# Three layer norms in a retention and mixture-of-experts kernel: rows broadcast ahead of the gate projection, a bf16 normalisation fed by POOL's casting loads, and an output normalisation on DVE alone

## The chip, the cores and the metric

The kernel runs on 8 cores of one Trainium2 chip. Every core works on 2048 tokens of its own and the cores exchange nothing. The metric is the device time of the slowest core in microseconds (us).

## What is computed

One layer: a linear retention with 16 heads, its layer norm and gate, then a mixture of 8 experts. Each half ends in a layer norm over the 2048 features. Cut to what matters:

```python
q = x @ Wq.T;  v = x @ Wv.T                    # heads of 128
ret = scan(state = lam * state + v)            # along the sequence
out = _layernorm(q * ret, gamma, beta)         # "LN1"
x1 = x + (out * silu(x @ Wg.T)) @ Wo.T
x1n = _layernorm(x1)                           # "LN2"
w = top-2 of sigmoid(x1n @ Wgate.T), normalised
h = silu(x1n @ W1[e].T) * (x1n @ W3[e].T) * w[:, e]     # 8 experts
out = _layernorm(x1n + sum_e h @ W2[e].T)      # "LN3"
```

The kernel adds in the last line what it keeps in `x1hbm`, x1 before its norm.

## The kernel before

Tokens lie along the free axis and features on the 128 partitions, so one core's 2048 tokens make 16 feature tiles. The work is done in two halves of 1024 tokens (`emit_half`, called twice), and each half in two chunks of 512 (`c`, `CW=512`). The program is written out as five lists of instructions, one for each engine, in the order in which Python emits them. Each engine runs its list in order and waits on semaphores. Nothing reorders them, so the place of a call in the source is its place in each engine's queue. POOL's queue carries both POOL's arithmetic and the loads that convert f32 to bf16; SP's queue carries plain loads and the stores of x1, ACT's the stores of the output.

A half goes through these stages:

- POOL loads all 16 tiles of `xnS` from `xfm` (line 471). `xnS` is first the bf16 input x, later the normalised x1.
- Wv (L492) and Wq (L563), 16 column groups each, 32 matmuls to a group. Weights come through `wringS`, a ring of 4 column tiles that `load_wcol` fills from POOL's queue (L226). ACT copies the Wv result out of PSUM banks 0 and 1 (L519), DVE runs the scan (L539) and multiplies (L575).
- LN1 statistics: sums and sums of squares by matmuls against a column of ones (L601, L609).
- `ln_rows` (L379 to L409): for each chunk, five short DVE instructions on one partition, a square root on ACT and a DVE reciprocal. It fills the rows `muR` and `rstdR`, 1x1024 each.
- Gate projection Wg: 16 groups (L631), silu on ACT into `ygS` (L644).
- `bcast_rows` (L423, L434; copies L429, L440): a matmul with a row of ones spreads each row over 128 partitions, and DVE copies it into `muB` and `rstdB`. It is called after the gate projection.
- DVE normalises: for each of 16 heads and 2 chunks one subtract (L658) and two multiplies (L664, L672), into `ygS`.
- Wo: 16 groups (L703), each reading all 16 tiles of `ygS`. DVE adds x (L716) from `xf32S` (loaded on SP, L690) into `x1tS`, which SP stores to `x1hbm` (L725). Statistics follow (L749, L758). `xf32S` and `x1tS` are rings of 4 tiles of 512.
- LN2: `ln_rows`, `bcast_rows`, then SP reloads x1 in f32 (L778), and a subtract (L784) and a multiply (L791) per tile and chunk write `xnS`, even tiles on DVE, odd ones on POOL. An all-engine barrier follows.
- Router (L833 and after), then four pairs of experts: W1 (L948), W3 (L966), W2 (L1020), with the sum kept in `x2S`.
- LN3: statistics (L1083, L1092), `ln_rows`, `bcast_rows`, then subtract (L1110) and multiply (L1117) per tile and chunk into `ot2S` (4 slots), even tiles on DVE, odd ones on POOL. ACT's queue stores the output (L1124).

Two waits matter at the seam between the halves. The `xnS` loads of the second half wait for the last read of `xnS` by W3, through `xn_b`; they stand in POOL's list behind whatever POOL has to do before them. And ACT's copy out of PSUM (L519) stands in ACT's list behind the 32 output stores.

Of the kernel before, what the change touches and what calls it, by code (L numbers as in the profile page):

```python
# [26 lines left out]
class Prog:  # L27

    def __init__(self, nc):
        self.nc = nc  # L30
# [4 lines left out]
        names += [f"dG{i}" for i in range(4)] + [f"dR{i}" for i in range(4)]
        names += [f"dW{i}" for i in range(4)] + [f"dA{i}" for i in range(2)]
        names += [f"out{i}" for i in range(4)]
        for s in names:
            self.sems[s] = nc.alloc_semaphore(s)
            self.counts[s] = 0  # L40
# [80 lines left out]
def build(TC=2048, PREF=6144, CW=512):  # L121
# [72 lines left out]
    xf32S = A("xf32S", [P, 4 * CW], F32)  # L194
# [19 lines left out]
    xfR = Ring(4)  # L214
    x1R = Ring(4)
# [4 lines left out]
    gbufB = [[Buf() for _ in range(FT)] for _ in range(2)]  # L220

# [195 lines left out]
    def bcast_rows(t_mu, t_rs, bank_a, bank_b):
        dmu = muB_b.begin_write()
        drs = rstdB_b.begin_write()
        toks = []  # L420
        for c in range(NCW):
            da = psB[bank_a].begin_write()
            tm = pr.tick("pe", lambda en, c=c, b=bank_a: en.matmul(  # L423
                out=psS[b][:, 0:CW], lhsT=onesrow_f[:],
                rhs=muR[:, c * CW:(c + 1) * CW], start=True, stop=True),
                deps=[t_mu[c], t_ones_f] + da + dmu)
# [16 lines left out]
            psB[bank_b].read(tbr)  # L443
            toks += [tbm, tbr]
# [8 lines left out]
    def emit_half(half, state_prev_half):  # L453
# [3 lines left out]
        with (  # L457
# [7 lines left out]
            nc.sbuf_tensor(f"x1tS{half}", [P, 4 * CW], F32) as x1tS,  # L465
# [153 lines left out]
            t_mu1, t_rs1 = ln_rows(st_sum + st_sq, 0, 2)  # L619
# [32 lines left out]
            bt1 = bcast_rows(t_mu1, t_rs1, 4, 5)  # L652
# [116 lines left out]
            t_mu2, t_rs2 = ln_rows(st2_sum + st2_sq, 4, 6)  # L769
            bt2 = bcast_rows(t_mu2, t_rs2, 6, 7)  # L770
# [3 lines left out]
            for kt in range(KT):  # L774
                eng = "dve" if kt % 2 == 0 else "pool"
                for c in range(NCW):
                    xslot, xbuf = xfR.next()
                    trb = pr.dma("sp", lambda en, kt=kt, c=c, xslot=xslot: en.dma_start(  # L778
                        out=xf32S[:, xslot * CW:(xslot + 1) * CW],
                        in_=x1hbm[kt * P:(kt + 1) * P, hoff + c * CW:hoff + (c + 1) * CW]),  # L780
                        deps=t_x1w_all + xbuf.begin_write(), sem=f"dR{xslot}")
                    xbuf.wrote(trb)
                    ntslot, ntbuf = ntR.next()
                    tn1 = pr.tick(eng, lambda en, xslot=xslot, c=c, ntslot=ntslot: en.tensor_tensor(  # L784
                        out=ntmpS[:, ntslot * CW:(ntslot + 1) * CW],
# [448 lines left out]
```

How the kernel before makes its waits and increments, by code:

```python
            def run(engobj):  # L70
                lastwait = {}
                for deps, action, inc, inc_by in self.steps[eng]:
                    for s, v in deps:
                        if lastwait.get(s, 0) < v:
                            engobj.wait_ge(self.sems[s], v)
                            lastwait[s] = v
                    ins = action(engobj)
                    if inc is not None:
                        ins.then_inc(self.sems[inc], inc_by)
```

## Time and profile before

| | us |
|---|---|
| median of 2 runs | 4744.77 (4743.55 to 4746.0) |
| the profiled execution | 4743.55 |
| its span on the slowest core (core 7) | 4741.9 |
| spans of the eight cores | 4731.9 to 4741.9 |
| PE busy | 3961.9 (84%) |
| DVE busy | 1210.7 (26%) |
| POOL busy | 510.3 (11%) |
| ACT busy | 351.2 (7%) |

The span runs from the first to the last instruction of a core; the profiled execution's time is 1.65 us above it. Busy shares are means over stages that have different limits. What the change touches lies in the short stretches in which PE stands still, so the views to read are the chain that ended last and the timeline at each of those stretches.

### The profile page before, as it was taken

What the parts mean: (1) busy time and instruction counts of PE and PEld (TensorE: products, weight loads), DVE (VectorE), ACT (ScalarE), POOL (GpSimd) and SP (SyncE); (2) the same over time, 40 slices, a digit from 0 to 9 for tenths busy, and PEclk for the clock granted to TensorE, in tenths of its full rate; (3) what the DMA queues carried; (4) which work ended last, traced back from release to release, by engine and by line L of the source; (5) the groups of instructions that cost most, each with busy time, mean ns of one, the idle gap of its engine ahead of it and who ended that gap; (6) DMA issues with size and microseconds to landing.
All of it is one profiled execution on the core that took longest, in us unless ns stands there. A gap on an engine that the chain in (4) does not pass through costs nothing.

```text
span 4741.9 us, 46603 instructions; the slowest of 8 cores (4731.9 to 4741.9 us)
## 1 busy us (share of the span) xinstructions
PE 3961.9 (84%) x17449; PEld 1698.8 (36%) x17449; DVE 1210.7 (26%) x1891; ACT 351.2 (7%) x622; POOL 510.3 (11%) x730
## 2 busy tenths in 40 slices
PE   5698848189999999999919984736999999999993
PEld 1243313034444444444404431312444444444441
DVE  0122061621211211112242216152121121121126
ACT  0002101000000000000100210100000000000001
POOL 2100000400000000000050000030000000000004
PEclk5699969599999999999959996967999999999996
DMA  9843325334744444444254331533465444444441
GB/s 161 132 74 53 65 53 133 102 58 71 137 80 71 78 72 71 72 71 76 49 124 76 67 54 28 136 115 58 71 113 99 71 78 71 72 76 71 72 75 71
DMA packets 132169, 388.99 MB, mean 82 GB/s; under 512 B 15216, under 2 KB 15216, under 8 KB 131952
## 3 DMA queue, kind: packets, MB, share of 16 engines
q0 software_dynamic: 85392, 302.06, 38.6%
q1 hardware_dynamic: 37344, 67.17, 4.8%
q10 hardware_dynamic: 9216, 16.78, 1.0%
q8 instruction: 147, 2.41, 0.2%
q14 instruction: 70, 0.57, 0.0%
HBM read 654.42 MB, written 33.55 MB: 145 GB/s over the span
## 4 chain that ended last, share of the span: by engine, by line
PE 79%; DVE 8%; DMA 4%; issue 4%; POOL 3%; ACT 2%; DVEq 0%; ACTq 0%; POOLq 0%; SPq 0%; PEldq 0%
PE ps L948 19%; PE ps L1020 19%; PE ps L966 19%; PE ps L631 5%; PE ps L492 5%; PE ps L563 5%; PE ps L703 4%; DMA wring<-xpre 2%; DMA wring<-wvT 1%; DVE ntmpS L664 1%; DVE ygS L672 1%; POOL ot2S L1110 1%; DVE x1tS L716 1%; DVE ntmpS L658 1%; PE ps L925 1%
## 5 line engine op out<-in xcount | busy, mean ns | idle before, releaser
L948 PE MATMUL ps<-xnS,wring 128*128 128x512 bf16 x4096 | 939.4, 389 | 0.0
L966 PE MATMUL ps<-xnS,wring 128*128 128x512 bf16 x4096 | 904.9, 379 | 0.0
L1020 PE MATMUL ps<-gbufS,wring 128*128 128x512 bf16 x4096 | 886.4, 379 | 0.0
L948 PEld LDWEIGHTS ps<-xnS,wring 128*128 128x128 bf16 x4096 | 407.6, 100 | 526.6 <-issue 66.7
L966 PEld LDWEIGHTS ps<-xnS,wring 128*128 128x128 bf16 x4096 | 400.8, 98 | 483.2
L1020 PEld LDWEIGHTS ps<-gbufS,wring 128*128 128x128 bf16 x4096 | 400.2, 98 | 484.9 <-issue 3.5
L989 DVE TENSOR_TENSOR gtmpS<-ps,sh1S 128x512 bf16<-128x512 f32 x256 | 175.9, 687 | 1470.1 <-PE ps L966 1470.1
L703 PE MATMUL ps<-ygS,wring 128*128 128x512 bf16 x1024 | 258.0, 409 | 122.8 <-DVE ygS L672 122.8
L492 PE MATMUL ps<-xnS,wring 128*128 128x512 bf16 x1024 | 231.3, 385 | 106.7 <-DMA wring<-wvT 106.7
L982 ACT ACTIVATE sh1S<-ps 128x512 bf16<-128x512 f32 x256 | 139.0, 594 | 2366.9 <-PE ps L948 2366.9
L631 PE MATMUL ps<-xnS,wring 128*128 128x512 bf16 x1024 | 236.6, 385 | 48.1 <-ACT ygS L644 30.9
L1045 DVE SCALAR_TENSOR_TENSOR x2S<-ps,x2S 128x512 f32<-128x512 f32 x192 | 132.8, 692 | 517.5 <-PE ps L1020 517.5
L563 PE MATMUL ps<-xnS,wring 128*128 128x512 bf16 x1024 | 226.2, 379 | 0.0
L703 PEld LDWEIGHTS ps<-ygS,wring 128*128 128x128 bf16 x1024 | 99.1, 101 | 276.5 <-issue 177.9
L492 PEld LDWEIGHTS ps<-xnS,wring 128*128 128x128 bf16 x1024 | 101.2, 99 | 232.6 <-issue 115.0
L998 DVE TENSOR_TENSOR gbufS<-ewbS,gtmpS 128x512 bf16<-128x512 f32 x256 | 177.2, 692 | 27.7 <-DVE gtmpS L989 1.4
L226 POOL DMA_DIRECT2D wring<-w1T x128 | 67.7, 529 | 999.3 <-PE ps L948 924.6
L631 PEld LDWEIGHTS ps<-xnS,wring 128*128 128x128 bf16 x1024 | 99.0, 99 | 185.3 <-issue 78.7
L226 POOL DMA_DIRECT2D wring<-w2T x128 | 67.5, 528 | 817.6 <-PE ps L1020 613.1
L226 POOL DMA_DIRECT2D wring<-w3T x128 | 67.6, 528 | 801.6 <-PE ps L966 701.7
L563 PEld LDWEIGHTS ps<-xnS,wring 128*128 128x128 bf16 x1024 | 98.9, 98 | 117.1
L328 PE MATMUL ps<-wring,preWb 128*16 128x512 bf16 x192 | 88.4, 614 | 60.7 <-DMA wring<-xpre 57.6
(130 smaller groups left out, 1655.7 us busy)
## 6 DMA issues: line engine op xcount, KB each, us to landing
wring<-w1T POOLq DMA_DIRECT2D x128, 512.0 KB, 5.1
wring<-w3T POOLq DMA_DIRECT2D x128, 512.0 KB, 5.1
wring<-w2T POOLq DMA_DIRECT2D x128, 512.0 KB, 5.0
xf32S<-x1hbm SPq DMA_DIRECT2D x128, 256.0 KB, 3.7
wring<-xpre POOLq DMA_DIRECT2D x48, 512.0 KB, 9.8
xf32S<-xfm SPq DMA_DIRECT2D x64, 256.0 KB, 6.9
wring<-wvT POOLq DMA_DIRECT2D x32, 512.0 KB, 6.1
wring<-wqT POOLq DMA_DIRECT2D x32, 512.0 KB, 6.1
```

The lines of the kernel that those rows point to most:

```text
L226: lambda en, t=wringS[s], sr=src_ap, X=X: en.dma_start(out=t[:, 0:X], in_=sr),
L492: grp = pr.step("pe", lambda en, kt=kt, c=c, slot=slot: en.matmul(out=psS[c][:, 0:CW], lhsT=wringS[slot][:, kt * P:(kt + 1) * P], rhs=xqS[ ...
L563: grp = pr.step("pe", lambda en, kt=kt, c=c, slot=slot: en.matmul(out=psS[2 + c][:, 0:CW], lhsT=wringS[slot][:, kt * P:(kt + 1) * P], rhs= ...
L631: grp = pr.step("pe", lambda en, kt=kt, c=c, slot=slot: en.matmul(out=psS[c][:, 0:CW], lhsT=wringS[slot][:, kt * P:(kt + 1) * P], rhs=xqS[ ...
L703: grp = pr.step("pe", lambda en, kt=kt, c=c, slot=slot: en.matmul(out=psS[2 + c][:, 0:CW], lhsT=wringS[slot][:, kt * P:(kt + 1) * P], rhs= ...
L948: g1 = pr.step("pe", lambda en, kt=kt, c=c, slot=slot1: en.matmul(out=psS[c][:, 0:CW], lhsT=wringS[slot][:, kt * P:(kt + 1) * P], rhs=x1nS ...
L966: g3 = pr.step("pe", lambda en, kt=kt, c=c, slot=slot3: en.matmul(out=psS[2 + c][:, 0:CW], lhsT=wringS[slot][:, kt * P:(kt + 1) * P], rhs= ...
L982: ts1 = pr.tick("act", lambda en, c=c, shslot=shslot: en.activation(out=sh1S[:, shslot * CW:(shslot + 1) * CW], in_=psS[c][:, 0:CW], func= ...
L989: tg1 = pr.tick("dve", lambda en, c=c, shslot=shslot, gtslot=gtslot: en.tensor_tensor(out=gtmpS[:, gtslot * CW:(gtslot + 1) * CW], in0=psS ...
L998: gd = pr.tick("dve", lambda en, ei=ei, ft=ft, c=c, gtslot=gtslot: en.tensor_tensor(out=gbufS[:, (ei * FT + ft) * TH + c * CW:(ei * FT + f ...
L1020: grp = pr.step("pe", lambda en, k=k, c=c, slot=slot2: en.matmul(out=psS[4 + c][:, 0:CW], lhsT=wringS[slot][:, k * P:(k + 1) * P], rhs=gbu ...
L1045: tx2 = pr.tick("dve", lambda en, ht=ht, c=c: en.scalar_tensor_tensor(out=x2S[:, ht * TH + c * CW:ht * TH + (c + 1) * CW], in0=psS[4 + c][ ...
```

## The change

`ln_rows` and `bcast_rows` become one function, `ln_rows_bcast`, that works chunk by chunk: rows of the chunk, its two broadcast matmuls, its two copies, then the next chunk. The rows shrink from 1x1024 to 1x512, so chunk 1 waits until chunk 0's matmuls have read them. For LN1 it is called before the gate projection instead of `ln_rows` there and `bcast_rows` behind. LN2 and LN3 now broadcast through banks 2 and 3.

LN2's normalisation reads x1 as bf16: POOL's queue loads it with conversion into `xcS` (ring of 4), two DVE casts make bf16 copies of `muB` and `rstdB`, and subtract and multiply run on DVE alone, all operands bf16. LN3's normalisation runs on DVE alone, still in f32. `xf32S` and `x1tS` go from 4 slots to 3.

```diff
+    def ln_rows_bcast(stat_toks, bank_sum, bank_sq, bank_a, bank_b):
...
         for c in range(NCW):
+            rowdep = rowsB.begin_write()
             tmu = pr.tick("dve", lambda en, c=c: en.tensor_scalar(
-                out=muR[:, c * CW:(c + 1) * CW],
-                in0=psS[bank_sum + c][0:1, 0:CW],
+                out=muR[:, 0:CW], in0=psS[bank_sum + c][0:1, 0:CW],
                 scalar1=1.0 / D, scalar2=None, op0=ALU.mult),
                 deps=list(stat_toks) + rowdep)
...
-            t_mu1, t_rs1 = ln_rows(st_sum + st_sq, 0, 2)
+            bt1 = ln_rows_bcast(st_sum + st_sq, 0, 2, 4, 5)
...
             xn_b.read(g_grp[NH - 1])
-            bt1 = bcast_rows(t_mu1, t_rs1, 4, 5)
...
+            bt2 = ln_rows_bcast(st2_sum + st2_sq, 4, 6, 2, 3)
+            t_mbb = pr.tick("dve", lambda en: en.tensor_copy(
+                out=muBb[:, 0:TH], in_=muB[:, 0:TH]), deps=bt2 + muB_b.begin_write() * 0)
+            t_rbb = pr.tick("dve", lambda en: en.tensor_copy(
+                out=rstdBb[:, 0:TH], in_=rstdB[:, 0:TH]), deps=bt2)
...
-                eng = "dve" if kt % 2 == 0 else "pool"
-                    trb = pr.dma("sp", lambda en, kt=kt, c=c, xslot=xslot: en.dma_start(
-                        out=xf32S[:, xslot * CW:(xslot + 1) * CW],
+                    trb = pr.dma("pool", lambda en, kt=kt, c=c, xcslot=xcslot: en.dma_start(
+                        out=xcS[:, xcslot * CW:(xcslot + 1) * CW],
                         in_=x1hbm[kt * P:(kt + 1) * P, hoff + c * CW:hoff + (c + 1) * CW]),
...
-                eng3 = "dve" if ht % 2 == 0 else "pool"
+                eng3 = "dve"
```

On PE, from the last LN1 statistics of the first half to the first Wo group, the four broadcast matmuls (`ps<-muR`, `ps<-rstdR`) stand behind the gate projection in the kernel before:

```order
L609 MATMUL ps<-sqS,onescol_bf 1x512
L631 MATMUL ps<-xnS,wring 128x512 x512
L423 MATMUL ps<-muR,onesrow_f 128x512
L434 MATMUL ps<-rstdR,onesrow_f 128x512
L423 MATMUL ps<-muR,onesrow_f 128x512
L434 MATMUL ps<-rstdR,onesrow_f 128x512
L703 MATMUL ps<-ygS,wring 128x512 x32
```

In the changed kernel they stand ahead of it (its own line numbers; L622 is the gate projection, L693 is Wo):

```order
L599 MATMUL ps<-sqS,onescol_bf 1x512
L412 MATMUL ps<-muR,onesrow_f 128x512
L423 MATMUL ps<-rstdR,onesrow_f 128x512
L412 MATMUL ps<-muR,onesrow_f 128x512
L423 MATMUL ps<-rstdR,onesrow_f 128x512
L622 MATMUL ps<-xnS,wring 128x512 x512
L693 MATMUL ps<-ygS,wring 128x512 x32
```

The gate's 512 matmuls moved behind both chunks' broadcast, and Wo follows them directly.

On POOL, at the seam between the halves, the kernel before has 32 LN3 instructions (16 such pairs, then line 471) between the last W2 loads and the next half's input:

```order
L226 DMA wring<-w2T 128x2048 x16
L1110 TENSOR_TENSOR ot2S<-x2S,muB 128x512
L1117 TENSOR_TENSOR ot2S<-ot2S,rstdB 128x512
L1110 TENSOR_TENSOR ot2S<-x2S,muB 128x512
L1117 TENSOR_TENSOR ot2S<-ot2S,rstdB 128x512
```

In the changed kernel the same place reads (L461 is the load of the input):

```order
L233 DMA wring<-w2T 128x2048 x16
L461 DMA xnS<-xfm 128x1024 x16
L233 DMA wring<-wvT 128x2048
L233 DMA wring<-wqT 128x2048
L233 DMA wring<-wvT 128x2048
L233 DMA wring<-wqT 128x2048
```

Nothing is left between the last W2 load and the second half's input.

On DVE, for LN1, the kernel before has the two copies of each chunk behind both chunks' rows:

```order
L409 RECIPROCAL rstdR<-rstdR 1x512
L379 TENSOR_SCALAR muR<-ps 1x512
L386 TENSOR_SCALAR msR<-ps 1x512
L392 TENSOR_TENSOR rstdR<-muR 1x512
L396 TENSOR_TENSOR msR<-msR,rstdR 1x512
L401 TENSOR_SCALAR msR<-msR 1x512
L409 RECIPROCAL rstdR<-rstdR 1x512
L429 COPY muB<-ps 128x512
L440 COPY rstdB<-ps 128x512
L429 COPY muB<-ps 128x512
L440 COPY rstdB<-ps 128x512
```

In the changed kernel chunk 0's copies come before chunk 1's rows (L418 and L429 are the copies):

```order
L409 RECIPROCAL rstdR<-rstdR 1x512
L418 COPY muB<-ps 128x512
L429 COPY rstdB<-ps 128x512
L387 TENSOR_SCALAR muR<-ps 1x512
L392 TENSOR_SCALAR msR<-ps 1x512
L397 TENSOR_TENSOR rstdR<-muR 1x512
L400 TENSOR_TENSOR msR<-msR,rstdR 1x512
L403 TENSOR_SCALAR msR<-msR 1x512
L409 RECIPROCAL rstdR<-rstdR 1x512
L418 COPY muB<-ps 128x512
L429 COPY rstdB<-ps 128x512
```

The DVE list is as long as before here; only two copies moved forward.

## Rows read from the trace of the kernel before

**Rows 1.** The page, part 4: shares of the chain that ended last, by engine.
```profile
PE 79%; DVE 8%; DMA 4%; issue 4%; POOL 3%; ACT 2%; DVEq 0%; ACTq 0%; POOLq 0%; SPq 0%; PEldq 0%
```
**Rows 2.** Waits: who waited for whom, us in total, times, longest.
```profile
PE ps L703 <- DVE ygS L672: 122.8, 32, 5.7
```
**Rows 3.** Timeline, start of the first half's gate projection: start us, us, engine, line.
```profile
443.55 0.68 DVE L379 TENSOR_SCALAR muR<-ps 1x512 f32<-1x512 f32 x1 [20.21 <-PE ps L609]
...
448.83 3.34 DVE L409 RECIPROCAL rstdR<-rstdR 1x512 f32<-1x512 f32 x1 [2.10 <-ACT rstdR L405]
452.10 0.62 DVE L379 TENSOR_SCALAR muR<-ps 1x512 f32<-1x512 f32 x1
...
452.96 8.39 PE L631 MATMUL ps<-xnS,wring 128*128 128x512 bf16 x31 [8.11 <-DVE muR L379]
...
456.03 3.34 DVE L409 RECIPROCAL rstdR<-rstdR 1x512 f32<-1x512 f32 x1 [0.82 <-ACT rstdR L405]
```
**Rows 4.** Timeline, LN2's broadcast matmul of the first half.
```profile
843.94 2.04 PE L434 MATMUL ps<-rstdR,onesrow_f 1*128 1x512 f32 x2 [6.44 <-DVE msR L386]
```
**Rows 5.** Timeline, last gate group of each half.
```profile
579.73 5.56 PE L631 MATMUL ps<-xnS,wring 128*128 128x512 bf16 x25
...
2862.38 7.23 PE L631 MATMUL ps<-xnS,wring 128*128 128x512 bf16 x32 [0.94 <-ACT ygS L644]
```
**Rows 6.** The chain in order of time, Wo groups: start us, us, what.
```profile
670.54 9.03 PE ps L703 x32
682.90 7.03 PE ps L703 x32
693.40 7.03 PE ps L703 x32
...
2958.49 8.53 PE ps L703 x32
```
**Rows 7.** Timeline, LN2's normalisation: its first DVE instructions and POOL's last.
```profile
855.01 0.68 DVE L784 TENSOR_TENSOR ntmpS<-xf32S,muB 128x512 f32<-128x512 f32 x1
...
856.41 0.68 DVE L784 TENSOR_TENSOR ntmpS<-xf32S,muB 128x512 f32<-128x512 f32 x1
...
909.01 1.26 POOL L791 TENSOR_TENSOR xnS<-ntmpS,rstdB 128x512 bf16<-128x512 f32 x1
```
**Rows 8.** Groups by line: busy us, mean ns, idle before.
```profile
L791 DVE TENSOR_TENSOR xnS<-ntmpS,rstdB 128x512 bf16<-128x512 f32 x32 | 48.3, 1509 | 3.3
...
L732 DVE CAST cbS<-x1tS 128x512 bf16<-128x512 f32 x64 | 27.3, 427 | 6.6
...
L316 DVE CAST preWb<-preW 128x768 bf16<-128x768 f32 x1 | 0.6, 560 | 2.2 <-ACT preW L311 2.2
```
**Rows 9.** DMA issues: out<-in, queue, count, KB written by each, median us to landing.
```profile
xf32S<-x1hbm SPq DMA_DIRECT2D x128, 256.0 KB, 3.7
...
wring<-wgT POOLq DMA_DIRECT2D x32, 512.0 KB, 5.1
wring<-woT POOLq DMA_DIRECT2D x32, 512.0 KB, 7.0
...
outfm<-ot2S ACTq DMA_DIRECT2D x64, 256.0 KB, 2.4
xnS<-xfm POOLq DMA_DIRECT2D x32, 256.0 KB, 16.8
```
**Rows 10.** Busy time by stretch: bounds, length, five engines, PEclk, DMA share, GB/s.
```profile
2444.60:2481.40 36.80, 0.00 (x0) 0.00 (x0) 0.00 (x0) 0.00 (x0) 10.60 (x21) 0.50 1.04 157
```
**Rows 11.** Timeline of the seam between the halves.
```profile
2320.17 0.53 POOL L226 DMA_DIRECT2D wring<-w2T  x1 [6.38 <-PE ps L1020]
...
2390.40 0.68 DVE L1110 TENSOR_TENSOR ot2S<-x2S,muB 128x512 f32<-128x512 f32 x1
...
2444.58 8.51 POOL L471 DMA_DIRECT2D xnS<-xfm  x16
...
2481.45 9.81 PE L492 MATMUL ps<-xnS,wring 128*128 128x512 bf16 x32 [91.76 <-DMA wring<-wvT]
...
2498.01 7.07 PE L492 MATMUL ps<-xnS,wring 128*128 128x512 bf16 x32
```
**Rows 12.** Timeline, the last arithmetic instruction of the kernel.
```profile
4737.39 1.26 POOL L1117 TENSOR_TENSOR ot2S<-ot2S,rstdB 128x512 f32<-128x512 f32 x1
```

More of the change, by code:

```diff
@@ L36, in __init__ @@
         names += [f"dW{i}" for i in range(4)] + [f"dA{i}" for i in range(2)]
+        names += [f"dC{i}" for i in range(4)]
         names += [f"out{i}" for i in range(4)]
@@ L193, in build @@
     xnS = A("xnS", [P, KT * TH], BF16)
-    xf32S = A("xf32S", [P, 4 * CW], F32)
+    xf32S = A("xf32S", [P, 3 * CW], F32)
+    muBb = A("muBb", [P, TH], BF16)
+    rstdBb = A("rstdBb", [P, TH], BF16)
+    xcS = A("xcS", [P, 4 * CW], BF16)
+    ntbS = A("ntbS", [P, 2 * CW], BF16)
     NWR = 4
@@ L417, in bcast_rows @@
[L417 to L421, printed above, removed]
+            tv1 = pr.tick("dve", lambda en: en.tensor_tensor(
+                out=rstdR[:, 0:CW], in0=muR[:, 0:CW], in1=muR[:, 0:CW],
+                op=ALU.mult), deps=[tmu])
+            tv2 = pr.tick("dve", lambda en: en.tensor_tensor(
+                out=msR[:, 0:CW], in0=msR[:, 0:CW], in1=rstdR[:, 0:CW],
+                op=ALU.subtract), deps=[tms, tv1])
@@ L424, in bcast_rows @@
                 out=psS[b][:, 0:CW], lhsT=onesrow_f[:],
[L425 to L426 removed]
+                rhs=muR[:, 0:CW], start=True, stop=True),
+                deps=[tmu, t_ones_f] + da + dmu)
             psB[bank_a].wrote(tm)
@@ L433, in bcast_rows @@
             db = psB[bank_b].begin_write()
-            tr = pr.tick("pe", lambda en, c=c, b=bank_b: en.matmul(
+            tr = pr.tick("pe", lambda en, b=bank_b: en.matmul(
                 out=psS[b][:, 0:CW], lhsT=onesrow_f[:],
-                rhs=rstdR[:, c * CW:(c + 1) * CW], start=True, stop=True),
-                deps=[t_rs[c], t_ones_f] + db + drs)
+                rhs=rstdR[:, 0:CW], start=True, stop=True),
+                deps=[trc, t_ones_f] + db + drs)
             psB[bank_b].wrote(tr)
@@ L464, in emit_half @@
             nc.sbuf_tensor(f"ntmpS{half}", [P, 2 * CW], F32) as ntmpS,
-            nc.sbuf_tensor(f"x1tS{half}", [P, 4 * CW], F32) as x1tS,
+            nc.sbuf_tensor(f"x1tS{half}", [P, 3 * CW], F32) as x1tS,
         ):
@@ L780, in emit_half @@
                         in_=x1hbm[kt * P:(kt + 1) * P, hoff + c * CW:hoff + (c + 1) * CW]),
[L781 to L785, printed above, removed]
-                        in0=xf32S[:, xslot * CW:(xslot + 1) * CW],
-                        in1=muB[:, c * CW:(c + 1) * CW], op=ALU.subtract),
-                        deps=[trb, muB_b.ready] + ntbuf.begin_write())
+                        deps=t_x1w_all + xcbuf.begin_write(), sem=f"dC{xcslot}")
@@ L789, in emit_half @@
+                    xcbuf.wrote(trb)
+                    ntslot, ntbuf = ntbR.next()
+                    tn1 = pr.tick("dve", lambda en, xcslot=xcslot, c=c, ntslot=ntslot: en.tensor_tensor(
+                        out=ntbS[:, ntslot * CW:(ntslot + 1) * CW],
+                        in0=xcS[:, xcslot * CW:(xcslot + 1) * CW],
+                        in1=muBb[:, c * CW:(c + 1) * CW], op=ALU.subtract),
+                        deps=[trb, t_mbb] + ntbuf.begin_write())
                     muB_b.read(tn1)
-                    xbuf.read(tn1)
@@ L1143, in build @@
         [f"dW{i}" for i in range(4)] + [f"dA{i}" for i in range(2)] + \
-        [f"out{i}" for i in range(4)]
+        [f"dC{i}" for i in range(4)] + [f"out{i}" for i in range(4)]
     final_deps = [(sname, pr.counts[sname]) for sname in dma_sems]
```

78 lines of the change are left out of this document (31 added, 47 removed).

## The prediction

> **What bounds the kernel now.** I read the chain of work that ended last first. PE holds 79% of it [rows 1], so most of the kernel is matmul that the change leaves alone, and only what lies between the matmul stages can give time. The list of waits names the first such place: PE's Wo matmuls waited 122.8 us for DVE's `ygS` [rows 2]. The timeline gives the rest. In each half PE stands still while LN2 is normalised (855.0 to 910.3 us, [rows 7]), and at the seam between the halves PE waits 91.76 us until 2481.45 [rows 11]. The end of the kernel is LN3 again, up to POOL's last instruction at 4738.65 [rows 12]. The change touches all four places, each twice or once. The sum is made against the profiled execution, 4743.55 us, which is 1.2 us below the median of the runs.
>
> **LN1: rows and broadcast ahead of the gate.** What it adds: PE may start the gate only after both chunks' rows and broadcasts. Rows of chunk 0 run from 443.55 to 452.17, 8.62 us; those of chunk 1 from 452.10 to 459.37, 7.27 us [rows 3]. Behind each comes a hand-over to PE (0.24 us, the gap between 452.72 and 452.96 in [rows 3]) and a pair of broadcast matmul passes at 2.04 us with PE at its lower clock [rows 4]; between chunks a copy of some 0.6 us starts before the next rows do, with 0.1 for its hand-over. So the gate starts at 443.55 + 8.62 + 0.24 + 2.04 + 0.7 + 7.27 + 0.24 + 2.04 = 464.7, against 452.96: 11.7 us later. The first group is slow now (8.39 for 31 matmuls) and stays so.
>
> What it removes: the last gate group ends at 585.3 and 2869.6 [rows 5], and the second Wo group starts only at 670.5 and 2958.4 [rows 6], since the first had to follow DVE through 16 heads. That chain takes at most (670.5 - 585.3) / 16 = 5.3 us a head. A gate group takes (585.3 - 453.0) / 16 = 8.3 us. With `muB` and `rstdB` there beforehand, DVE normalises head by head under the gate, which covers it with 3 us to spare each. Behind the last gate group remain its silu (about 1.1 us) and one head, at most 6.4 us, and the first Wo group wants the last head after 15/16 of its 6.9 us: no stall, or a fraction of one. The second Wo group then starts at gate end + 6.9 + 3.5 (groups are 10.5 apart and 7.03 long, [rows 6]). First half: 585.3 + 11.7 + 10.4 = 607.4 instead of 670.5, 63.1 saved. Second half: 2869.6 + 11.7 + 10.4 = 2891.7 instead of 2958.4, 66.7 saved. The group there runs 9.03 and 8.53 today and should run 7.03 with PE not having stopped: 2.0 and 1.5 more. **LN1 gives 133.3 us.** If the cover failed altogether, it would give nothing but its cost.
>
> **LN2.** Rows and broadcasts end within 1 us of before, since chunk 0's copies are overlapped differently: I get 855.9 against 855.1. The two casts of 1024 columns are new. A cast of 512 takes 427 ns and one of 768 takes 560 [rows 8], so one of 1024 about 0.69; the first subtract moves from 855.0 to about 857.1. Today 32 tiles take until 910.3 because DVE and POOL slow each other: the multiply that is done in about 0.7 us alone (a whole pair takes 856.41 - 855.01 = 1.40 us, [rows 7]) has a mean of 1509 ns when both run [rows 8].
>
> No row shows a subtract with all operands bf16. Its bounds are the cast's 0.43 us and half of the f32 pair, 0.70. I take 0.43, because the cast too handles bf16 on one side and runs at the faster rate; then a dependent pair costs about 0.87 with its gap and 32 tiles cost 28 us. At the other bound they cost 32 x 1.40 = 44.8.
> The Trainium skill (VectorE: DVE Perf Modes, "The perf-mode tier table") says a tensor_tensor on bf16 in SBUF runs at twice the rate of f32. By that rule the sum is the one I make; by the f32 row alone it would be 18 us longer.
>
> The loads are the likelier limit. The ring has 4 slots, and slot i is refilled by POOL only after the subtract of tile i. The nearest rows: 256 KB on SP's queue land in 3.7 us, 512 KB with conversion on POOL's queue in 5.1 [rows 9]. The new load reads as many bytes as the first and writes half. I take 3.7. A slot's turn is then 0.43 + 3.7 + 0.2 for two hand-overs = 4.3 us for four tiles, 1.1 a tile, 35 us for 32: slower than DVE's 0.87, so it decides. LN2 ends at 857.1 + 35.5 = 892.6 instead of 910.3. **LN2 gives 17.6 us a half, 35.2 in all**, between 8 (f32 speed, or landing at 5.1 us: 46 us) and 25 (paced by DVE) a half.
>
> **The seam.** LN3's DVE work starts at about 2391.2 instead of 2390.4, for the same reason as in LN2. DVE alone needs 32 x 1.40 = 44.8 us [rows 7] and ends at 2436.0. A slot of `ot2S` must be free three tiles (4.2 us) after its store was released, and the store lands in 2.4 us [rows 9]: no wait. What counts more is POOL. Its last W2 load is issued at 2320.17 and it has nothing left before the second half's input loads, which today start at 2444.58 behind its share of LN3 [rows 11]. Those loads keep the DMA engines full for 36.8 us [rows 10]. Started at about 2321 they are in by about 2360, and the Wv and Wq weights follow as the ring frees. Nothing that W2 still needs is queued behind them. So PE goes straight from LN3's broadcast (2390.3) into the first Wv and Wq groups (9.8 and 6.9 us), under DVE's LN3. The third group needs banks 0 and 1, which ACT empties only after its last output store: 2436.0 + 0.9 + 1.1 = 2438.0. It starts today at 2498.01 [rows 11]. From 60.0 I take 2.9 because PE has stopped again and that group runs at 9.8 instead of 6.9. **The seam gives 57.1 us.** Were the loads not earlier, only LN3's own 8.6 us would remain.
>
> **The end.** LN3 of the second half today runs 54.2 us from its first DVE instruction to POOL's last, as in the first half. At 44.8, started 0.8 later, it saves **8.6 us**; the tail of 3.3 us behind it stays.
>
> **Costed at nothing.** The rings of 3: SP reloads `xf32S` in program order behind the previous group's stores, by when the slot in question has been read. `x1tS` slots come round every 11.6 us at the tightest, and stores land within 8; a late one would cost 1 or 2 us, up to 5 over the kernel. In the expert stage a tile takes 3.5 us and three slots give 10 us for a 3.7 us load.
>
> **Sum.** 133.3 + 35.2 + 57.1 + 8.6 = 234.2 saved; 4743.55 - 234.2 = 4509.4 us, 4.9% less. About 2% is what a measurement of this kernel can tell from no change.
>
> **Rivals.** *Casting loads slow down under DVE.* The same POOL queue lands a Wo weight in 7.0 us while DVE casts are running, a gate weight in 5.1 [rows 9]. At 7.0 a turn is 7.6 us, 1.9 a tile, 61 us a half: LN2 ends 8 us later than today instead of 18 earlier, and the total is 4561. Against it: four small loads in flight, and the Wo stage has SP's traffic beside it.
> The Trainium skill (SBUF — State Buffer, "SBUF: two separate sides") describes exactly this, a POOL-issued DMA whose descriptors can't be written while DVE holds both ports in a fast mode, and puts a 620 ns DMA at 3100 ns. By that rule the time is this rival's; but it names copies, and the two-input subtract here may not hold both ports.
>
> *The seam stays shut.* If the input loads or ACT still hold PE until after LN3, the seam gives 8.6 instead of 57.1: 4558. The order of the lists speaks against it.
>
> *The gate does not hide DVE.* Then LN1 gives nothing: about 4643. The spare of 3 us a head speaks against it.
>
> *Slower: POOL's loads queue up.* The input loads on the same queue have a median landing of 16.8 us [rows 9] with 16 of them queued. At 16.8 a tile of LN2 costs 4.4 us, a half 139 instead of 53, and the total is 4743.55 - 199 + 172 = 4717, within 2%. The point from which the kernel is slower is a tile of 4.8 us, a landing of 18.5. At 30 us it would be 7.6 a tile and 244 a half: 4927. With four loads in flight, not sixteen, I hold it unlikely.
>
> **How the numbers follow.** Forecast 0.70, with its own range 4488 to 4535 (LN2 at 25 or at 8 a half, a few us on the seam). Slow casting loads 0.12, shut seam 0.08, gate does not hide 0.02, landing near 17 us 0.04, slower 0.02, the rest spread. The range goes from 4486 to 4562 and so takes in the first two rivals. Faster by over 2% is below 4650: 0.94; within 2% 0.04; slower 0.02.
>
> **What would show it.** In the profile after: the wait of Wo on DVE's `ygS` should fall from 122.8 us to a few; the gate should start some 21 us behind the first LN1 row; LN2's bf16 instructions should show near 0.43 us and DVE waiting for `xcS` about 1 us in four tiles; the input loads of the second half should be issued some 25 us before the last W2 group ends, and PE should do two groups, stop some 30 us, and go on right behind DVE's last LN3 instruction. LN3's multiply should be at 0.7 us instead of 1.5. I am wrong if `xcS` lands above 5 us, or if DVE waits for output stores in LN3.

## The result, and the profile after

The changed kernel is faster: the ratio to the kernel before is 0.956, 95% interval 0.953 to 0.959. That is 4529.2 us at the lowest against 4742.0, some 213 us less; the prediction said 234. (In some executions of either kernel the cores of one die run at a lower clock; such runs are left out of the ratio and of everything below.) The profiled execution took 4537.75 us, and its slowest core is core 2.

From the page of the changed kernel: span, busy time of the engines, and the chain that ended last.

```profile
span 4536.2 us, 46515 instructions; the slowest of 8 cores (4521.0 to 4536.2 us)
...
PE 3950.1 (87%) x17449; PEld 1701.4 (38%) x17449; DVE 1176.7 (26%) x2023; ACT 351.4 (8%) x622; POOL 351.9 (8%) x666
...
PE 82%; DVE 6%; DMA 6%; issue 3%; ACT 2%; POOL 0%; DVEq 0%; ACTq 0%; SPq 0%; PEldq 0%; POOLq 0%
```

PE's share of the chain rose from 79% [rows 1] to 82%, DVE's and POOL's fell, and DMA's rose from 4% to 6%. A part of that is new: the page now lists `DMA xcS<-x1hbm`, LN2's loads, with 1% of the chain.

To see where the time went I cut both spans at the same six events, the first row instruction of each later norm (DVE's `muR<-ps`). In the timeline it stands at 443.55, 833.93, 2369.32, 2726.94, 3127.25 and 4663.33 us before, and at 447.36, 780.33, 2309.03, 2612.36, 2941.32 and 4466.27 after. The differences give the stages:

| stage | before | after | saved | predicted |
|---|---|---|---|---|
| start to LN1, first half | 443.6 | 447.4 | -3.8 | 0 |
| LN1 to LN2 (gate, Wo), first half | 390.4 | 333.0 | 57.4 | 63.1 |
| LN2 to LN3, first half | 1535.4 | 1528.7 | 6.7 | 17.6 |
| LN3 to LN1 (seam) | 357.6 | 303.3 | 54.3 | 57.1 |
| LN1 to LN2, second half | 400.3 | 329.0 | 71.4 | 66.7 |
| LN2 to LN3, second half | 1536.1 | 1525.0 | 11.1 | 17.6 |
| LN3 to the end | 78.6 | 69.9 | 8.6 | 8.6 |
| sum (the spans) | 4741.9 | 4536.2 | 205.7 | 230.7 |

The prediction's LN1 term holds another 3.5 us for Wo groups that no longer run slow, which makes its sum 234.2. Of the 28.5 us that are missing, LN2 holds 17.4, LN1 4.5, the start 3.8 and the seam 2.8.

Waits of the changed kernel (who waited for whom, us in total, times, longest):

```profile
DVE ygS L662 <- ACT ygS L635: 133.4, 32, 10.2
...
DVE ntbS L779 <- DMA xcS<-x1hbm: 28.2, 26, 3.2
...
DVE ot2S L1104 <- DMA outfm<-ot2S: 3.5, 3, 2.6
```

PE's wait for `ygS` of DVE, 122.8 us in [rows 2], is gone from the list. Now DVE waits for ACT's silu, 133.4 us, which costs nothing: it shows that DVE keeps up under the gate. The second line is the new cost, DVE waiting 28.2 us for LN2's input.

Timeline of the changed kernel from LN1 to Wo in the first half (start us, us, what, idle before):

```profile
447.36 0.68 DVE L387 TENSOR_SCALAR muR<-ps 1x512 f32<-1x512 f32 x1 [20.18 <-PE ps L599]
...
466.46 2.04 PE L423 MATMUL ps<-rstdR,onesrow_f 1*128 1x512 f32 x2 [4.62 <-DVE rstdR L409]
...
468.44 9.83 PE L622 MATMUL ps<-xnS,wring 128*128 128x512 bf16 x32
...
480.49 8.90 PE L622 MATMUL ps<-xnS,wring 128*128 128x512 bf16 x32 [2.22 <-ACT ygS L635]
...
490.34 7.23 PE L622 MATMUL ps<-xnS,wring 128*128 128x512 bf16 x32 [0.94 <-ACT ygS L635]
...
603.71 7.07 PE L693 MATMUL ps<-ygS,wring 128*128 128x512 bf16 x32
...
614.00 8.74 PE L693 MATMUL ps<-ygS,wring 128*128 128x512 bf16 x32
```

The gate starts 21.1 us behind the first row instruction (447.36 to 468.44), as predicted, against 9.4 before [rows 3]. Wo starts in the same instant as the gate ends, and its second group 10.3 us later. But two gate groups are slow, 9.83 and 8.90 us, where before only the first was, 8.39 [rows 3]. That holds for the first half alone. In the second half the kernel before has two slow groups as well:

```profile
2735.08 9.08 PE L631 MATMUL ps<-xnS,wring 128*128 128x512 bf16 x31 [6.83 <-DVE muR L379]
2746.39 8.75 PE L631 MATMUL ps<-xnS,wring 128*128 128x512 bf16 x32 [2.22 <-ACT ygS L644]
```

The changed kernel has 10.00 and 8.92 us there. Busy time by stretch of the changed kernel's first half shows the clock (bounds, length, five engines, then the granted clock, DMA share and GB/s):

```profile
468.50:480.00 11.50, 9.77 (x33) 3.67 (x32) 2.04 (x3) 1.64 (x2) 0.53 (x1) 0.76 0.00 0
480.50:490.00 9.50, 8.89 (x32) 3.41 (x32) 4.21 (x6) 0.74 (x3) 0.00 (x1) 0.82 0.29 55
490.40:600.00 109.60, 97.25 (x431) 41.14 (x432) 57.49 (x83) 14.29 (x27) 7.00 (x14) 1.00 0.39 67
```

1.00 is the 2.4 GHz level; 0.76 and 0.82 are means of a stretch that was partly at 1.2. Ahead of it PE had done only two short broadcasts a chunk for 21 us.

Groups by line (busy us, mean ns, idle before) and DMA issues (KB written by each, median us to landing) of the changed kernel:

```profile
L1111 DVE TENSOR_TENSOR ot2S<-ot2S,rstdB 128x512 f32<-128x512 f32 x64 | 44.3, 692 | 7.0 <-DVE ot2S L1104 0.5
...
L786 DVE TENSOR_TENSOR xnS<-ntbS,rstdBb 128x512 bf16<-128x512 bf16 x64 | 27.2, 425 | 7.0 <-DVE ntbS L779 0.5
...
L779 DVE TENSOR_TENSOR ntbS<-xcS,muBb 128x512 bf16<-128x512 bf16 x64 | 27.0, 421 | 28.6 <-DMA xcS<-x1hbm 28.2
...
L761 DVE CAST muBb<-muB 128x1024 bf16<-128x1024 f32 x2 | 1.4, 694 | 0.2
```
```profile
outfm<-ot2S ACTq DMA_DIRECT2D x64, 256.0 KB, 2.6
...
xcS<-x1hbm POOLq DMA_DIRECT2D x64, 128.0 KB, 4.3
```

The prices of the DVE instructions are the ones taken: 421 and 425 ns for the bf16 pair (0.43), 694 for the cast of 1024 columns (0.69), 692 for LN3's multiply (0.7). The landing is 4.3 us where 3.7 was taken.

LN2 of the changed kernel, first half:

```profile
780.33 0.68 DVE L387 TENSOR_SCALAR muR<-ps 1x512 f32<-1x512 f32 x1 [0.93 <-PE ps L748]
...
803.59 0.41 DVE L779 TENSOR_TENSOR ntbS<-xcS,muBb 128x512 bf16<-128x512 bf16 x1
...
804.58 0.53 POOL L773 DMA_DIRECT2D xcS<-x1hbm  x1 [20.35 <-DVE xnS L786]
...
805.44 0.53 POOL L773 DMA_DIRECT2D xcS<-x1hbm  x1 [0.33 <-DVE xnS L786]
...
808.64 0.43 DVE L779 TENSOR_TENSOR ntbS<-xcS,muBb 128x512 bf16<-128x512 bf16 x1 [1.52 <-DMA xcS<-x1hbm]
...
811.40 0.43 DVE L779 TENSOR_TENSOR ntbS<-xcS,muBb 128x512 bf16<-128x512 bf16 x1 [1.80 <-DMA xcS<-x1hbm]
...
848.86 0.42 DVE L786 TENSOR_TENSOR xnS<-ntbS,rstdBb 128x512 bf16<-128x512 bf16 x1
...
850.80 1.44 PE L828 MATMUL ps<-xnS,wgfS 128*8 128x512 bf16 x3 [49.33 <-PEq L65]
```

The first tile stands 23.3 us behind the first row instruction, as worked out. Then 32 tiles take 803.59 to 849.28, 45.7 us, 1.43 each instead of 1.1. (In the second half they take 41.5 us, 1.30 each.) The lines show why. The subtract of tile 0 ends at 804.00, but its slot's new load is issued at 804.58, 0.58 later. (The trace names the multiply, which ends at 804.52, as what released it; in the program the load waits for the subtract. What the 0.58 us go into isn't shown.) Tile 4 uses that load at 808.64, 4.1 us after the issue; tile 5 uses the next one, issued at 805.44, only at 811.40, 6.0 us after. Tile 5 waits for that late load, and the tiles behind it wait with it, since the ring is read in order.

The seam of the changed kernel, POOL's input loads first:

```profile
2260.12 8.45 POOL L461 DMA_DIRECT2D xnS<-xfm  x16
...
2309.03 0.68 DVE L387 TENSOR_SCALAR muR<-ps 1x512 f32<-1x512 f32 x1 [1.38 <-PE ps L1087]
...
2330.12 9.13 PE L482 MATMUL ps<-xnS,wring 128*128 128x512 bf16 x32
...
2339.09 7.07 PE L553 MATMUL ps<-xnS,wring 128*128 128x512 bf16 x32
...
2378.79 0.69 DVE L1111 TENSOR_TENSOR ot2S<-ot2S,rstdB 128x512 f32<-128x512 f32 x1
2380.00 1.07 ACT L509 COPY vS<-ps 128x512 f32<-128x512 f32 x2 [55.55 <-DVE ot2S L1111]
...
2380.83 9.36 PE L482 MATMUL ps<-xnS,wring 128*128 128x512 bf16 x32 [34.68 <-ACT vS L509]
```

This is the predicted order: the input loads follow the last W2 load, two groups run under LN3, PE stops for 34.7 us and goes on right behind LN3's last instruction and ACT's copy.

### The profile page after: what moved, and what is told of

Same layout as the page of the kernel before. It is cut to its first block, busy times and chain, and to the rows that moved or that the text cites. A ratio compares the mean times of both kernels' runs of the same rounds, so it can differ in the third digit from the quotient of the medians.

```text
span 4536.2 us, 46515 instructions; the slowest of 8 cores (4521.0 to 4536.2 us)
## 1 busy us (share of the span) xinstructions
PE 3950.1 (87%) x17449; PEld 1701.4 (38%) x17449; DVE 1176.7 (26%) x2023; ACT 351.4 (8%) x622; POOL 351.9 (8%) x666
## 4 chain that ended last, share of the span: by engine, by line
PE 82%; DVE 6%; DMA 6%; issue 3%; ACT 2%; POOL 0%; DVEq 0%; ACTq 0%; SPq 0%; PEldq 0%; POOLq 0%
PE ps L943 20%; PE ps L1015 20%; PE ps L961 19%; PE ps L622 5%; PE ps L693 5%; PE ps L482 5%; PE ps L553 5%; DMA wring<-xpre 2%; DMA xcS<-x1hbm 1%; DVE x1tS L706 1%; DVE rstdR L409 1%; PE ps L920 1%; DVE ot2S L1104 1%; DMA wring<-wvT 1%; PE ps L423 1%
## 5 line engine op out<-in xcount | busy, mean ns | idle before, releaser
L482 PE MATMUL ps<-xnS,wring 128*128 128x512 bf16 x1024 | 233.3, 387 | 53.9 <-ACT vS L509 34.7
L622 PE MATMUL ps<-xnS,wring 128*128 128x512 bf16 x1024 | 239.9, 389 | 31.2 <-ACT ygS L635 31.0
L693 PE MATMUL ps<-ygS,wring 128*128 128x512 bf16 x1024 | 237.8, 393 | 0.0
L622 PEld LDWEIGHTS ps<-xnS,wring 128*128 128x128 bf16 x1024 | 100.0, 100 | 173.0 <-issue 68.4
L693 PEld LDWEIGHTS ps<-ygS,wring 128*128 128x128 bf16 x1024 | 100.5, 100 | 130.4 <-issue 23.3
```

The lines of the kernel that those rows point to most:

```text
L482: grp = pr.step("pe", lambda en, kt=kt, c=c, slot=slot: en.matmul(out=psS[c][:, 0:CW], lhsT=wringS[slot][:, kt * P:(kt + 1) * P], rhs=xqS[ ...
L622: grp = pr.step("pe", lambda en, kt=kt, c=c, slot=slot: en.matmul(out=psS[c][:, 0:CW], lhsT=wringS[slot][:, kt * P:(kt + 1) * P], rhs=xqS[ ...
L693: grp = pr.step("pe", lambda en, kt=kt, c=c, slot=slot: en.matmul(out=psS[2 + c][:, 0:CW], lhsT=wringS[slot][:, kt * P:(kt + 1) * P], rhs= ...
```

## The experiments

Each is read by its ratio to the kernel before and by the stage times cut as above.

**One part at a time.** `ln1_only`:

```diff
             t_mu1, t_rs1 = ln_rows(st_sum + st_sq, 0, 2)
+            bt1 = bcast_rows(t_mu1, t_rs1, 4, 5)
...
             xn_b.read(g_grp[NH - 1])
-            bt1 = bcast_rows(t_mu1, t_rs1, 4, 5)
```

> The kernel before, with one edit: LN1's broadcast stands right behind its rows, ahead of the gate. Theory (the gate covers DVE's heads): 125 to 133 us less than before, a ratio of 0.972 to 0.974, and the second Wo group at about 610 us instead of 670.5. Rival (part of the time that the whole change gained came from elsewhere, the gate hides only some of it): under 100 us less, ratio above 0.979, and PE in Wo still waits tens of us for ygS of DVE.

Measured: 0.973 (0.969 to 0.977), 4614.7 at the lowest against 4746.0, 131 us less. Its second Wo group:

```profile
610.01 8.59 PE L703 MATMUL ps<-ygS,wring 128*128 128x512 bf16 x32
```

The theory holds. Moving one call gives over half of the whole gain.

`ln3_only`:

```diff
-                eng3 = "dve" if ht % 2 == 0 else "pool"
+                eng3 = "dve"
```

> The kernel before, with one edit: LN3's subtract and multiply run on DVE alone. Theory (POOL's list is empty at the seam, so the second half's loads and its first two matmul groups lie under LN3): 62 to 66 us less, ratio 0.986 to 0.987. Rival (only DVE's faster instructions count): twice 5 to 9 us, 10 to 18 us less, ratio 0.996 to 0.998.

Measured: 0.985 (0.981 to 0.990), 70 us less (4675.9 against 4746.0). The stage from LN3 to LN1 took 306.5 us (core 2) against 357.6. Of the rest, 10 us lie in the end and 7 in the second half's LN1 stage, which this edit doesn't touch. The rival, that only the faster instructions count, is out.

`input_early` separates what is in that number. LN3 stays split over both engines; only the 16 input loads move ahead of it in POOL's list:

```diff
+    def load_input(hoff):
+        xn_dep = xn_b.begin_write()
+        for kt in range(KT):
+            pr.dma("pool", ... out=xnS[...], in_=xfm_d[...] ...)
...
+            if half == 0:
+                load_input(TH)
```

> The kernel before, with LN3 still split over DVE and POOL, but the second half's 16 input loads stand in POOL's list ahead of LN3's arithmetic. Theory (their place in POOL's list is what the seam pays): PE waits for the input no longer, 40 to 50 us less, ratio 0.990 to 0.992; the weights of Wv and Wq are still behind POOL's arithmetic, which may hold back up to 20 us of it. Rival (the seam pays because DVE is alone on LN3): 0 to 10 us less, ratio 0.998 to 1.000.

Measured: 4713.1 us in one run against 4746.0, so 33 less (no interval). That is less than the theory's 40 to 50 and far above the rival's 10. The trace is of another run, with a mean granted clock of 0.82 on this core, but the stretch read here holds no full matmul group, whose length would hang on the clock. POOL's list in it, and PE's first group:

```profile
2666.06 8.47 POOL L454 DMA_DIRECT2D xnS<-xfm  x16
...
2796.86 0.60 POOL L226 DMA_DIRECT2D wring<-wvT  x1
```
```profile
2804.63 9.55 PE L496 MATMUL ps<-xnS,wring 128*128 128x512 bf16 x32 [62.76 <-DMA wring<-wvT]
```

From LN3's first row instruction (2721.50 in this trace) to that group are 83.1 us, against 112.1 before. So 29 us come from the input loads' place in POOL's list, as the theory says, and PE then waits 62.8 us for the first Wv weight, which is issued behind POOL's share of LN3. The seam's gain has two parts: input loads earlier, 29, and weight loads and ACT's copy no longer behind a slow LN3, the other 25.

**What LN2's new form is worth.** `after_ln2_old` is the changed kernel with LN2's f32 way back:

```diff
-                    trb = pr.dma("pool", ... out=xcS[...], in_=x1hbm[...] ...)
+                    trb = pr.dma("sp", ... out=xf32S[...], in_=x1hbm[...] ...)
...
+                eng = "dve" if kt % 2 == 0 else "pool"
```

> The changed kernel with LN2's normalisation as before (f32 loads on SP's queue, DVE and POOL, no bf16 copies of the rows). If LN2 gave what the two traces say, about 7 and 11 us a half, this kernel takes about 18 us more than the changed one, a ratio to before of about 0.960. If it gave what was predicted, 35 us, the ratio is about 0.9635. If it gave nothing, 0.956.

Measured: 0.963 (0.959 to 0.967), 4568.8 at the lowest. The interval holds the first and the second case and can't choose between them; by the lowest times it is 38 us above the changed kernel (4531.3 in its own repetition below), where the stage times of the two main traces give 18. The trace gave the reason: from LN2's first row instruction to the router it took 89.0 and 87.0 us on core 3, and 82 to 88 on cores 0 to 2, where the kernel before took 77.4 and 78.0. My experiment had kept the rings at three slots, and the f32 way reads from that very ring. So it was done again with four slots in both rings (`after_ln2_old_r4`):

```diff
-    xfR = Ring(3)
-    x1R = Ring(3)
+    xfR = Ring(4)
+    x1R = Ring(4)
```

> The changed kernel with LN2's normalisation as before and with the two rings back at four slots. The run with three slots came out 38 us above the changed kernel, where the stage times of the two main traces gave 18 to 21. Theory (three slots slow the f32 way of LN2: 89 and 87 us from its first row instruction to the router, against 77.4 and 78.0 with four slots before the change): here it takes 77 to 78 again, and the kernel 18 to 21 us more than the changed one, ratio to before 0.960 to 0.961. Rival (the reading of the stages misses something, and the bf16 way is worth 38 us in itself): ratio 0.963 to 0.964 as with three slots.

Measured: 0.960 (0.958 to 0.962), 4551.5 at the lowest, 20 us above the changed kernel (4531.3 in its own repetition below). Its LN2, first half:

```profile
780.40 0.68 DVE L387 TENSOR_SCALAR muR<-ps 1x512 f32<-1x512 f32 x1 [0.93 <-PE ps L748]
...
858.62 1.86 PE L822 MATMUL ps<-xnS,wgfS 128*8 128x512 bf16 x4 [57.07 <-PEq L65]
```

78.2 us, and 78.8 in the second half, about as before the change. So LN2's new form is worth about 20 us, and three slots instead of four cost the old form 17 by the lowest times, 19 by the stages of the slowest core. In the changed kernel the smaller rings cost nothing that shows: DVE waits for `xf32S<-xfm` in Wo twice, 17.7 us together, against twice and 18.9 before.

**Why LN2 gave less than predicted.** `after_ring8` doubles the loads in flight:

```diff
-    xcR = Ring(4)
+    xcR = Ring(8)
```

> The changed kernel with eight slots instead of four in the ring that feeds LN2. Theory (LN2 is paced by a slot's turn: hand-over to POOL, landing, hand-over back; in the changed kernel 1.43 us a tile): with twice the loads in flight DVE sets the pace at 0.87 us a tile, 28 us for 32 tiles instead of 45.7, DVE's waits for xcS nearly gone, 30 to 35 us less than the changed kernel over both halves, ratio to before about 0.949. Rival (the loads are limited by bandwidth or by POOL writing their descriptors beside a running DVE, so more in flight land later each): tiles stay near 1.4 us, landing rises from 4.3 to about 8 us, ratio 0.956 as the changed kernel.

Measured: 0.953 (0.945 to 0.961), 4505.3 at the lowest. The interval is wide, since of its four runs three took 4505.3 to 4510.1 us and one 4567.8. So the trace has to decide: the stages from LN2 to LN3 are 1512.4 and 1511.1 us long against 1525.5 and 1525.2 in the changed kernel's repetition, 27 less together, a little under the 30 to 35 expected. The wait, the landing and the two ends of LN2 in this kernel:

```profile
DVE ntbS L779 <- DMA xcS<-x1hbm: 2.9, 4, 1.4
```
```profile
xcS<-x1hbm POOLq DMA_DIRECT2D x64, 128.0 KB, 6.0
```
```profile
796.72 0.42 DVE L779 TENSOR_TENSOR ntbS<-xcS,muBb 128x512 bf16<-128x512 bf16 x1
...
825.40 0.42 DVE L786 TENSOR_TENSOR xnS<-ntbS,rstdBb 128x512 bf16<-128x512 bf16 x1
```

DVE's waits fall from 28.2 to 2.9 us and 32 tiles take 29.1 us, 0.91 each (30.6 in the second half). The theory holds for the pace. The rival is half right: the landing does rise, from 4.3 to 6.0 us, while the data rate rises; which of the rival's two reasons is behind that isn't shown. Busy time by stretch during LN2's tiles, first of the changed kernel, then of this one:

```profile
804.00:849.00 45.00, 0.00 (x0) 0.00 (x0) 25.14 (x63) 0.00 (x0) 14.78 (x28) 0.50 0.75 82
```
```profile
797.00:825.00 28.00, 0.00 (x0) 0.00 (x0) 23.72 (x63) 0.00 (x0) 12.66 (x24) 0.50 0.89 113
```

The last two columns go from a DMA share of 0.75 and 82 GB/s to 0.89 and 113. With eight slots that just fits under DVE's pace, by an estimate from these figures: eight tiles of 0.87 us are 7.0 us, and a subtract, the hand-over to POOL and a landing, 0.43 + 0.58 + 6.0, are 7.0 too.

`x1_in_sbuf` takes the reload away altogether. The bf16 copy of x1 that the statistics need is written into `xnS`, and LN2 normalises in place:

```diff
-                        out=cbS[:, cbslot * CW:(cbslot + 1) * CW],
+                        out=xnS[:, mt * TH + c * CW:mt * TH + (c + 1) * CW],
...
-                        in0=xcS[:, xcslot * CW:(xcslot + 1) * CW],
+                        in0=xnS[:, kt * TH + c * CW:kt * TH + (c + 1) * CW],
```

> The changed kernel without LN2's reload: Wo's bf16 copy of x1, which the statistics read, is written into xnS (the input x is dead by then), and LN2 normalises xnS in place. Theory (only the reload holds LN2 up): DVE-paced at 0.87 us a tile, 28 us a half, 30 to 36 us less than the changed kernel, ratio to before about 0.949. Rival (DVE's bf16 pair itself is what takes 1.4 us a tile): no change, 0.956.

Measured: 0.948 (0.945 to 0.951), 4497.2 to 4511.5 us in five runs. From the first row instruction to the router it is 52.1 us (778.24 to 830.36 in its timeline), against 70.5 in the changed kernel. The theory holds: the bf16 pair runs at DVE's pace, 27.8 us for 32 tiles, once nothing has to be fetched.

`after_again` is the changed kernel itself, run beside these.

> The changed kernel itself once more, on the chip of this group of runs, so that its variants can be read against it: ratio 0.953 to 0.959 as before.

It gave one run to compare, 4531.3 us, and so no ratio; with a lowest run of before of 4743.6 on that chip it is 0.955. Its start took 445.1 us instead of 447.4, and LN2 gave 20.8 us in its trace.

**Going further.** `x1_in_sbuf_ones` replaces the column of ones by a 128x128 matrix of ones. The sums then stand on all partitions, `ln_rows_bcast` works on all of them at once, and no row is broadcast:

```diff
-    onescol_bf = A("onescol_bf", [P, 1], BF16)
+    onescol_bf = A("onescol_bf", [P, P], BF16)
...
-                        out=psS[c][0:1, 0:CW], lhsT=onescol_bf[:],
+                        out=psS[c][:, 0:CW], lhsT=onescol_bf[:],
```

> As x1_in_sbuf, and the statistics of all three norms by a 128x128 matrix of ones, so that the sums land on all 128 partitions and the broadcast matmuls and their copies go away. Theory (the 21 to 23 us between a norm's first row instruction and its first tile are a chain of dependent steps, of which two broadcasts with hand-overs and four copies, about 10 us, go): 50 to 60 us less than x1_in_sbuf over six norms, ratio about 0.937. Rival (a reciprocal or scale on 128 partitions costs more than on one, or the wide statistics matmuls cost PE more): under 20 us less, ratio 0.945 or above.

Measured: 0.930 (0.927 to 0.934), 4419.4 at the lowest, 78 us less than `x1_in_sbuf`. That is better than the theory, so it was run once more for its trace.

> x1_in_sbuf_ones once more, beside its skewed version: ratio 0.927 to 0.934 as before. It gained 78 us over x1_in_sbuf, not 50 to 60. If each norm's first row instruction to first tile fell from 23.3 us to about 12 (14 us with LN2's two casts), that is 6 x 11 = 66 us; the rest should be PE's clock, granted higher behind the shorter stops: the broadcasts are gone, and the first groups behind a stop then show less than 8.5 to 9.8 us each.

Measured: 4422.1 us in one run. LN1 and LN2 of its first half:

```profile
442.75 0.69 DVE L388 TENSOR_SCALAR muB<-ps 128x512 f32<-128x512 f32 x1 [20.18 <-PE ps L579]
...
446.43 8.54 PE L602 MATMUL ps<-xnS,wring 128*128 128x512 bf16 x31 [2.32 <-DVE muB L388]
...
448.22 6.56 DVE L414 RECIPROCAL rstdB<-rstdB 128x512 f32<-128x512 f32 x2
```
```profile
751.01 0.69 DVE L388 TENSOR_SCALAR muB<-ps 128x512 f32<-128x512 f32 x1 [0.93 <-PE ps L725]
...
764.36 0.42 DVE L750 TENSOR_TENSOR ntbS<-xnS,muBb 128x512 bf16<-128x512 bf16 x1
```

LN2's and LN3's first tile comes 13.4 and 11.9 us behind the first row instruction instead of 23.3 and 21.9, 10 us less each, as the theory said. The rest is in LN1, where I had been wrong: without broadcasts PE has no business in the chain, and the gate's first full group starts 3.7 us behind the first row instruction instead of 21.1, 17.4 us less. Twice 17.4 and four times 10 are 75 of the 78. That is a sum over the chains. The stages of the two traces agree with it only roughly: against `x1_in_sbuf` the two from LN1 to LN2 are 38 us shorter, the two from LN2 to LN3 13, the seam 13, the end 10 and the start, which the edit doesn't touch, 5. The clock is hardly in it: the first gate groups show 8.54 (31 of 32 matmuls) and 8.92 us, of which only the first is quicker than the changed kernel's 9.83 and 8.90.

`ones_skew2` moves the statistics in Wo behind the next group, alternates Wo's PSUM banks and gives both rings four slots again. As `ones_r4_skew` it did not fit in SBUF, where `ot2S` needs 8192 bytes and 8000 were left; `ones_skew2` is the same without five tiles that nothing uses any more. Its main edit:

```diff
+                for p in pend:
+                    stats2(*p)
+                pend = []
...
-                    st2_sum[c] = pr.step("pe", ...)
+                    pend.append((mt, c, tc_, tq_, sqslot, sqbuf))
```

> A version meant to be faster than both: x1_in_sbuf_ones with rings of four, and in the Wo stage each group's statistics matmuls stand behind the next group's 32 matmuls instead of ahead of them (PSUM banks alternate between 2, 3 and 0, 1). In Wo a group is 7.1 us of matmul every 10.5, since PE waits for the add, the cast and the square of the group it has just done. Theory (that wait goes, the statistics take 1.2 to 1.5 us a group): a group every 8.6 us, 1.9 x 15 x 2 = 57 us less than x1_in_sbuf_ones, ratio about 0.918. Rival (the stage moves 1.5 MB a group and its loads, not PE, then set the pace, as the 9 us waits for x of the changed kernel hint): under 20 us less, ratio 0.926 or above.

Measured: 0.920 (0.918 to 0.921), 4357.7 at the lowest, 62 us less than `x1_in_sbuf_ones` and 386 less than the kernel before. Groups of Wo, and DVE's wait for x:

```profile
599.10 7.07 PE L688 MATMUL ps<-ygS,wring 128*128 128x512 bf16 x32
...
606.87 7.07 PE L688 MATMUL ps<-ygS,wring 128*128 128x512 bf16 x32
```
```profile
DVE x1tS L704 <- DMA xf32S<-xfm: 165.3, 29, 10.2
```

The gain is the theory's, and the rival is right in part. A group takes 7.8 us where nothing is late, less than the 8.6 expected, but DVE now waits 165 us for x, and at intervals a group comes 11 us after the last. The loads are what the stage is up against next. How much of the 62 us the fourth slots give wasn't tried alone.

## Why the prediction was right or wrong

*LN1.* Right, 128.8 measured against 133.3, and 131 for that edit alone. The start of the gate at 21.1 us, the cover, the second Wo group 10.4 us after the gate's end all came as worked out. What failed is the step "the first group is slow now and stays so": in the first half the first group became slower and the second slow too, (9.83 - 8.39) + (8.90 - 7.23) = 3.1 us, and the gate as a whole lasted 2.9 us longer. Also the second Wo group still runs at 8.74 us, not at 7.03 "with PE not having stopped". The first half fell 5.7 us short of 63.1: the 2.9 of the gate, and 2.9 more from the second Wo group on, where one more group than before ran slow (8.74 to 8.77 us, against 7.08) and some groups started late, up to 11.6 us behind the last instead of 10.5. The second half came out 4.7 better than 66.7. There Wo had two slow groups less than before (three against five of 8.3 to 8.8 us) and fewer late ones. The granted clock of a slow Wo group is below 1.00 in both kernels: 0.81 over 614.00 to 623.00 in the changed one, 0.84 over 746.00 to 757.00 in the one before. Why a group in the midst of Wo gets less clock isn't shown. That the misses of the two halves nearly cancel is luck.

*LN2.* The mechanism was named rightly, a slot's turn and not DVE sets the pace, but the term was mis-sized: 17.8 us in this trace, 20 by the runs, instead of 35.2. The step that failed is "a slot's turn is 0.43 + 3.7 + 0.2 for two hand-overs = 4.3". The hand-over from DVE to POOL alone is 0.58, and the landing is 4.3 in the median. That makes 0.43 + 0.58 + 4.3 = 5.3 us, 1.33 a tile, and 1.30 to 1.33 is what the second half of this trace and both halves of the repetition show. The first half of this trace, at 4 x 1.43 = 5.7, is the slowest of the four; late loads, up to 6.2 us, would account for its rest, since in a ring read in order an early load gives nothing back. `after_ring8` shows that it is the turn, `x1_in_sbuf` that it is nothing else. The range's end, a landing of 5.1, gave 8 a half, which is about what came (6.7 and 11.1), but in part by luck: the landing was 4.3, and the hand-overs cost 0.4 more than was allowed.

The rival of casting loads that slow down under DVE did not come: 4.3 us, not 7.0. In `after_ring8` POOL issued a load about every 0.87 us beside a DVE that was busy almost without a break. The Trainium skill (SBUF — State Buffer, "SBUF: two separate sides") ties the starved descriptors to DVE's modes with two ports, and lets an instruction with two SBUF inputs block only a GpSimd instruction that reads SBUF. So the prediction had stretched that rule to an instruction that it doesn't name, and the trace doesn't speak against the page. The Trainium skill's other rule (VectorE: DVE Perf Modes, "The perf-mode tier table"), bf16 at twice the rate of f32, comes out in its direction: 421 ns against 684 for the f32 subtract of LN3, 1.6 times as fast.

*The seam.* Right, 54.3 against 57.1, and the mechanism as written. LN3 itself took 48.6 us (2330.90 to 2379.48) and not 44.8, mainly because DVE waited 3.3 us for output stores, which the prediction had excluded: "no wait". A store lands in 2.6 us in the median, but the latest took 6.6, more than the 4.2 us that the ring allows. The prediction had named such a wait as a sign that it is wrong. The trace of before would have told: there too DVE waits for those stores, 9.4 us in all, at a median landing of 2.4. `input_early` splits the term into 29 for the input's place in POOL's list and 25 for the rest. I had said that the input loads are what counts; they are half of it.

*The end.* 8.6 against 8.6.

*The start.* 3.8 us longer, though nothing in it was changed. The traces settle it. The same start took 442.1 us in `after_ring8`, 445.1 in the repetition and 448.2 in `x1_in_sbuf`, and 444.2 and 446.9 on two cores of `ln3_only`, which begins as the kernel before. It is spread between executions and cores.

*Costed at nothing.* Rightly, though one reading was off: the stores of x1 landed within 10.1 us in the trace before, not within 8. The changed kernel shows no wait for a slot of `x1tS`.

## What to carry to other kernels

A ring fed by DMA has a pace of its own: the consumer's instruction, the hand-over and the landing, divided by the number of slots. Take the landing from the queue that will be used, allow for the late ones (here 3.3 to 6.2 us around a median of 4.3), and compare with the consumer's time per tile; where they are near, double the slots, or ask whether the data must leave SBUF at all. Where engines run their lists in order, look at what stands ahead of a load in its queue before looking at the load: moving one call of LN1 gave 131 us, and 29 of the seam's 54 came from the place of 16 loads. And an experiment that undoes one part must also give it back its buffers.

## What was not expected of the hardware

- A reciprocal over 128 partitions and 512 columns took 3.32 us in the median (`ones_again`), the same as over one partition (3.34 in [rows 3]). A scale by a constant of 512 columns took 0.69 against 0.67. Work on a single row cost DVE what work on all partitions costs.
- A stop of PE is paid for twice: after 21 us with little work, the gate's first two groups took 9.83 and 8.90 us at a granted clock of 0.76 and 0.82, against 7.23 at 1.00. A shorter stop spared little of that. Behind 8 to 9 us the kernel before shows 8.39 and 7.23 in one half, 9.08 and 8.75 in the other; behind 3.7 us `ones_again` shows 8.54 and 8.92.
- The landing of a load isn't a property of the load: the same 128 KB took 4.3 us in the median with four in flight and 6.0 with eight.
